# Masked maximum of a graph layer: the own part added graph by graph, the update and the statistics cut in halves, the own products moved to the last selection

## What is computed

```python
m1z = z @ W1.T + b1
m2z = z @ W2.T + b2
pair = relu(m1z[:, :, None, :] + m2z[:, None, :, :])
m = max(where(mask, pair, -inf), axis=2)
x = x + relu(concatenate((z, m), axis=-1) @ Wu.T + bu)
```

## Time and profile before

| | us |
|---|---|
| median of three runs | 2116.69 |
| lowest and highest of them | 2104.98 and 2117.04 |
| the profiled execution | 2111.06 |
| its span | 2109.2 |
| the stretch of `phase_maxpass` from its first `reduce` to its last | 157.06 to 635.93 |

### The profile page before, as it was taken

How to read it: one execution, slowest core, us unless ns; L and a number is a source line. 1 busy time by engine, 2 the same in 40 slices (tenths; PEclk the granted TensorE clock), 3 DMA queues, 4 the chain that set the end, 5 groups by cost and what they waited for, 6 DMA issues and landing times. The chain is left out here.

```text
span 2109.2 us, 43810 instructions
## 1 busy us (share of the span) xinstructions
PE 1749.2 (83%) x13754; PEld 1106.5 (52%) x13771; DVE 1721.6 (82%) x2689; ACT 1396.4 (66%) x3229; POOL 593.0 (28%) x449
## 2 busy tenths in 40 slices
PE   2967677777776899996899999999999588888886
PEld 1855566566563666665465555555555144444445
DVE  5978888888885777875899999999998577777777
ACT  0533333333334989995588888888888577777774
POOL 1530000000002545443354444544444111111110
PEclk9978988988887999999999999999999899999999
DMA  6000000000000000000255555555555899999993
GB/s 180 1 13 1 1 0 0 0 0 0 0 1 4 7 6 6 4 7 21 81 220 225 223 219 224 219 224 220 226 221 219 324 340 344 344 339 341 338 330 87
DMA packets 123567, 292.98 MB, mean 139 GB/s; under 512 B 21376, under 2 KB 57608, under 8 KB 123288
## 3 DMA queue, kind: packets, MB, share of 16 engines
q1 hardware_dynamic: 106360, 283.37, 36.1%
q10 hardware_dynamic: 16896, 8.39, 1.4%
q0 software_dynamic: 256, 0.56, 0.1%
HBM read 150.45 MB, written 141.82 MB: 139 GB/s over the span
## 5 line engine op out<-in xcount | busy, mean ns | idle before, releaser
L1316 POOL TENSOR_TENSOR pair_ring<-hd 128x2048 f32 (+1 forms) x64 | 269.5, 4212 | 310.7 <-DVE pair_ring L1341 310.7
L1401 ACT ACTIVATE v_hid<-v_psW 128x1024 f32<-128x1024 f32 x256 | 263.4, 1029 | 85.2 <-PE v_psW L1439 85.2
L771 DVE TENSOR_REDUCE m_part<-m_psS 128x128 f32<-128x2048 f32 (+1 forms) x128 | 258.9, 2022 | 74.6 <-PE m_psS L638 74.6
L1337 DVE TENSOR_TENSOR pair_ring<-v_psX,hd 128x2048 f32<-128x2048 f32 x128 | 292.2, 2286 | 17.7 <-PE v_psW L1439 17.6
L1439 PE MATMUL v_psW<-pair_ring,p_w1T 128*64 128x512 f32 x1024 | 288.9, 597 | 0.0
L1404 ACT ACTIVATE v_junk<-v_psW 128x1024 bf16<-128x1024 f32 x256 | 263.3, 1029 | 0.0
L638 PE MATMUL m_psS<-m_onehot,m_tableT 32*128 32x128 f32 x3584 | 156.4, 314 | 125.4 <-DVE m_part L771 119.0
L1439 PE MATMUL v_psW<-pair_ring,l_w1T 128*64 128x512 f32 (+1 forms) x1024 | 252.5, 587 | 0.0
L1430 PE MATMUL v_psW<-p_ends,v_weights 128*64 128x512 bf16 x1536 | 235.2, 381 | 3.2 <-DMA v_fold<-in_c_fold_dram 3.2
L1587 DVE SCALAR_TENSOR_TENSOR pair_ring<-pair_ring 128x1024 f32<-128x1024 f32 x128 | 156.4, 1225 | 65.9 <-ACT pair_ring L1654 65.9
L638 PEld LDWEIGHTS m_psS<-m_onehot,m_tableT 32*128 32x128 f32 x3584 | 132.5, 213 | 145.2 <-issue 76.9
(11 more groups left out here) (260 smaller groups left out, 3360.5 us busy)
## 6 DMA issues: line engine op xcount, KB each, us to landing
pair_hidden<-v_hid SPq DMA_DIRECT2D x256, 512.0 KB, 2.6
pair_ring<-pair_hidden SPq DMA_DIRECT2D x128, 1024.0 KB, 7.4
adj_ring<-in_adj_dram ACTq DMA_DIRECT2D x16, 256.0 KB, 5.7
x_all<-in_x_dram ACTq DMA_DIRECT2D x16, 256.0 KB, 5.8
out_dram<-x_all SPq DMA_DIRECT2D x16, 256.0 KB, 2.3
pair_scores<-s_rot SPq DMA_DIRECT2D x64, 32.0 KB, 5.1
s_fwd<-pair_scores SPq DMA_DIRECT2D x64, 32.0 KB, 5.1
s_wide<-pair_scores SPq DMA_DIRECT2D x64, 32.0 KB, 5.5
```

The costliest lines, as they stand in the source:

```text
L771: nc.vector.tensor_reduce(part[:, i % 2, r, :], psS[:, :, 0:w].rearrange("z q (c i) -> z i q c", i=N), AX.XY, ALU.max).then_inc(reduced, 1)
L1316: nc.gpsimd.tensor_tensor(D[:, home(u, SLABS - 1), :].rearrange("c (h d i) -> c h d i", h=2, i=N), one, far, ALU.subtract).then_inc(psub_d ...
L1337: nc.vector.tensor_tensor(slab(s), own, windows(hd, n, s)[1], ALU.max).then_inc(max_done, 1)
L1401: nc.scalar.activation(hid[:, s, :], psW[:, buf, :], ACT.Identity, accum_out=hsum[:, bass.ds(m, 1)]).then_inc(evacuated, 1)
```

## The change

- `add_own` is done for one graph at a time, behind that graph's `merge` (behind `reduce` 1, 3, 5 and 7) in the same quad, instead of once behind `reduce` 0 of the next quad.
- VectorE's `update` is cut in two halves of 256 columns, behind the LATE tables of `reduce` 4 and 6; the first signals a new semaphore `half_added`, the second `added`.
- `statistics` takes two graphs at a time and moves one quad later: behind `reduce` 0 and 2 of the quad after.
- TensorE's `own` moves from behind `select` 5 to behind `select` 7.
- `quads` writes out four quads instead of two, and loops 6 times over two quads. The end of the phase changes with it.

```diff
-            quad(0, 0, False, True)
-            with eng.Fori(0, QUADS // 2 - 1) as t:
+            quad(0, 0, False, True, False)
+            quad(1, 1, True, True, False)
+            with eng.Fori(0, QUADS // 2 - 2) as t:
                 for u in (0, 1):
-                    quad(2 * t + (u + 1), 1 - u, True, True)
-            quad(QUADS - 1, 1, True, False)
+                    quad(2 * t + (u + 2), u, True, True, True)
+            quad(QUADS - 2, 0, True, True, True)
+            quad(QUADS - 1, 1, True, False, True)
...
-                        if at == 5:
+                        if at == 7:
                             own(g, p)
...
-                def add_own(g, p):
-                    dve.wait_ge(merged, done(g * G + (G - 1)))
-                    dve.wait_ge(mT_ready, done(g - 1))
-                    nc.vector.tensor_tensor(both[:, :], mx[:, :], m1[:, p, :], ALU.add).then_inc(summed, 1)
-
-                def update(g):
+                def add_own(g, p, i):
+                    dve.wait_ge(merged, done(g * G + i))
+                    if i == 0:
+                        dve.wait_ge(m1_copied, done(g))
+                        dve.wait_ge(mT_ready, done(g - 1))
+                    last = nc.vector.tensor_tensor(both[:, b(i)], mx[:, b(i)], m1[:, p, b(i)], ALU.add)
+                    if i == G - 1:
+                        last.then_inc(summed, 1)
+
+                def update(g, half):
                     dve.wait_ge(u_mm, done(g))
-                    xs = k.x[:, bass.ds(g * QC, QC)]
-                    nc.vector.scalar_tensor_tensor(out=xs, in0=psU[:, :], scalar=0.0, in1=xs, op0=ALU.max,
-                                                   op1=ALU.add).then_inc(added, 1)
-
-                def statistics(g):
-                    dve.wait_ge(added, done(g))
-                    ln_stats(nc, k, g)
+                    at = half * (QC // 2)
+                    xs = k.x[:, bass.ds(g * QC + at, QC // 2)]
+                    nc.vector.scalar_tensor_tensor(out=xs, in0=psU[:, at:at + QC // 2], scalar=0.0, in1=xs, op0=ALU.max,
+                                                   op1=ALU.add).then_inc(added if half else half_added, 1)
+
+                def statistics(g, half):
+                    dve.wait_ge(added if half else half_added, done(g))
+                    for i in (2 * half, 2 * half + 1):
+                        nc.vector.bn_stats(k.stats[:, bass.ds(g * G + i, 1), :], k.x[:, bass.ds((g * G + i) * C, C)])
...
                         if at == 0:
-                            if prev:
-                                add_own(g - 1, 1 - p)
                             tables(g, p, 2, LATE)
+                            if older:
+                                statistics(g - 2, 0)
                         if at == 1:
                             merge(g, 0)
                             tables(g, p, 3, EARLY)
+                            add_own(g, p, 0)
                         if at == 2:
                             tables(g, p, 3, LATE)
+                            if older:
+                                statistics(g - 2, 1)
...
                         if at == 4:
-                            if prev:
-                                update(g - 1)
                             if next:
                                 tables(g + 1, 1 - p, 0, LATE)
+                            if prev:
+                                update(g - 1, 0)
                         if at == 5:
                             merge(g, 2)
                             if next:
                                 tables(g + 1, 1 - p, 1, EARLY)
+                            add_own(g, p, 2)
+                        if at == 6:
+                            if next:
+                                tables(g + 1, 1 - p, 1, LATE)
                             if prev:
-                                statistics(g - 1)
-                        if at == 6 and next:
-                            tables(g + 1, 1 - p, 1, LATE)
+                                update(g - 1, 1)
...
-                add_own(QUADS - 1, 1)
-                update(QUADS - 1)
-                statistics(QUADS - 1)
+                for half in (0, 1):
+                    statistics(QUADS - 2, half)
+                for half in (0, 1):
+                    update(QUADS - 1, half)
+                for half in (0, 1):
+                    statistics(QUADS - 1, half)
```

More of the change, by code:

```diff
@@ L544, in phase_maxpass @@
             "grown", "tabled", "t_turned", "tT_ready", "match_mm", "onehot_ready"))
-        selected, reduced, merged, summed, mT_ready, own_mm, u_mm, added = (sem(n) for n in (
-            "selected", "reduced", "merged", "summed", "mT_ready", "own_mm", "u_mm", "added"))
+        selected, reduced, merged, summed, mT_ready, own_mm, u_mm, half_added, added = (sem(n) for n in (
+            "selected", "reduced", "merged", "summed", "mT_ready", "own_mm", "u_mm", "half_added", "added"))
         b = lambda i: slice(i * N, (i + 1) * N)
@@ L654, in update, with quad @@
                     last.then_inc(u_mm, 1)
-                def quad(g, p, prev, next):
+                def quad(g, p, prev, next, older):
                     for at in range(ITEMS):
@@ L739, in _ @@
             def _(dve):
-                for s in (tabled, reduced, merged, summed, added):
+                for s in (tabled, reduced, merged, summed, half_added, added):
                     dve.sem_inc(s, BIAS)
@@ L778, in merge, with quad @@
                     nc.vector.tensor_tensor(mx[:, b(i)], part[:, i % 2, 0, :], part[:, i % 2, 1, :], ALU.max).then_inc(merged, 1)
-                def add_own(g, p):
-                    dve.wait_ge(merged, done(g * G + (G - 1)))
-                    dve.wait_ge(mT_ready, done(g - 1))
-                    nc.vector.tensor_tensor(both[:, :], mx[:, :], m1[:, p, :], ALU.add).then_inc(summed, 1)
-                def update(g):
-                    dve.wait_ge(u_mm, done(g))
-                    xs = k.x[:, bass.ds(g * QC, QC)]
-                    nc.vector.scalar_tensor_tensor(out=xs, in0=psU[:, :], scalar=0.0, in1=xs, op0=ALU.max,
-                                                   op1=ALU.add).then_inc(added, 1)
-                def statistics(g):
-                    dve.wait_ge(added, done(g))
-                    ln_stats(nc, k, g)
+                def add_own(g, p, i):
[7 more added lines that the diff above has]
+                def update(g, half):
+                    dve.wait_ge(u_mm, done(g))
+                    at = half * (QC // 2)
[6 more added lines that the diff above has]
+                        nc.vector.bn_stats(k.stats[:, bass.ds(g * G + i, 1), :], k.x[:, bass.ds((g * G + i) * C, C)])
                 EARLY, LATE = range(BLK - 2), range(BLK - 2, BLK)
-                def quad(g, p, prev, next):
+                def quad(g, p, prev, next, older):
                     for at in range(ITEMS):
@@ L813, in quad @@
                                 tables(g + 1, 1 - p, 0, EARLY)
+                            add_own(g, p, 1)
                         if at == 4:
-                            if prev:
-                                update(g - 1)
                             if next:
                                 tables(g + 1, 1 - p, 0, LATE)
+                            if prev:
+                                update(g - 1, 0)
                         if at == 5:
@@ L830, in quad @@
                                 tables(g + 1, 1 - p, 2, EARLY)
+                            add_own(g, p, 3)
                 for i in range(2):
```

## The result

The changed kernel takes 2118.57 us (median of 16 runs), the kernel before 2108.92 (16 runs by then, 7.8 us under the median of the first three). The ratio is 1.0049, with a 95% interval of 1.0028 to 1.007: half a per cent slower. The forecast was a small gain. The time lies in the range, the direction is wrong. One later execution of the kernel before took 6273.40 us, three times the others, and stands in no ratio.

A forecast was written before the change was run, and what follows sets the result against it. The prediction took the loop between `select` and `reduce`, and the clock, as the bound. Terms -2.1 - 2.1 - 2.1 - 0.6 = -6.9 us gave 2104 from the profiled execution or 2110 from the median; it took 2110, range 2086 to 2128.

The forecast's parts named there:

- Step 0: VectorE in step 0: `add_own` out (0.60 us), two `bn_stats` in (0.45); -2.1 us, GpSimd meeting's 0.85 us left in.
- Quarter additions and halves: VectorE: quarter additions hidden in steps 1, 3, 5, 7 (+16 us if not); half `update`s about 0.35 us each.
- Step 4: With half an `update`, step 4 becomes select-bound at 3.44 us: 48.2 against 50.26, -2.1 us.
- Step 5: Without `own`: 8 of 14 at 4.15 us, 6 at 3.21; 52.5 us against 70.12.
- Own at full clock and its wait: Step 7 with `own`: 3.50 us at full clock, plus 0.35 waiting for the second half of `update`: 3.85.
- Own at low clock: Step 7 with `own`: 5.04 + 0.35 = 5.40 us in 10 of 14, 3.85 in 4; 69.4 us against 53.92.
- the last rival: `own` wholly at low clock in every quad: step 7 at 6.66 us, +18 more, kernel 2145 us; chance 0.05.
- The rival that named the low clock throughout steps 5 to 7: Clock low in steps 5 to 7 of each quad: 4.15 + 4.05 + 5.40, 190.4 us, kernel 2127; chance 0.16.

The follow-up runs named there:

- the idle products: Changed kernel plus three unread bf16 products of 512 columns behind `prepare` in each of steps 4, 5 and 6: 2083.20 us, ratio 0.9881 to the kernel before.
- `own` alone: Kernel before with one edit, `own` behind `select` 7 instead of `select` 5: 2124.17 us, ratio 1.0062.
- the wide bias product: Changed kernel with `own`'s bias product over all 128 rows (identity times bias) instead of one row: 2118.24 us, ratio 1.0046.
- the half `update` ahead: Changed kernel with the second half of `update` ahead of the LATE tables behind `reduce` 6: 2116.62 us, ratio 1.0022.
- all but `own`, `update` ahead: Changed kernel with `own` back behind `select` 5 and `update` whole, ahead of the LATE tables behind `reduce` 4: 2102.58 us, ratio 0.9964.
- before with idle products: Kernel before plus three unread bf16 products of 512 columns behind `prepare` in each of steps 4, 6 and 7: 2077.42 us, ratio 0.9846.

## Why the prediction was wrong

**The bound** (the loop of `select` and `reduce`, and the clock) was read rightly; the idle products show that the clock alone is worth 35 us of stretch in the kernel before.

**Step 0.** Forecast 57.4, measured 54.62 us: `add_own` went out as said, and less time was lost beside GpSimd than the 0.85 us I had left in: in the quad at 305.85 the LATE tables take 1.38 us, 0.54 over their 0.84. Step 3 fell by 1.3 us, unforeseen and not explained here.

**Quarter additions and halves.** Right: they are hidden. In the changed kernel VectorE is busy 2.88 of 3.13 us in step 3, and the version with everything but the move is faster than before. The Trainium skill, "VectorE: DVE Perf Modes", section on the TRN2 errata, advises against small tiles; by its formula a quarter takes 291 ns. The trace agrees with the length, 286 ns on average, but no cost of it is exposed here.

**Step 4.** Forecast 48.2, measured 51.20. The step is select-bound as said, and with the idle products it takes 48.20; but the low clock reaches back into `select` 5. I had let the fall start only in step 5.

**Step 5.** Forecast 52.5, measured 53.68. The nearness is in part luck: 11 of 14 were slow, not 8, and both lengths came out shorter than taken (up to 4.06 instead of 4.15, 3.14 instead of 3.21). The share was too low here as well.

**Own at full clock and its wait.** Right in both: 3.50 forecast, 3.60 measured; 0.35 and 0.37 for the wait.

**Own at low clock: the step that failed.** The prediction put "10 slow of 14" at 5.40, 69.4 us. It was 14 of 14 at a mean of 5.79, 81.00 us, and this 11.6 us is more than the whole forecast gain. Two terms are in it.

The share: I counted the clock's falls from a kernel with one light step ahead of `own` and carried the count over, with a little off, to one with three. The text said that the cover was thinner and then took a lower share than the 12 of 14 it had read; the rows gave no reason for that. Four more slow steps are 4 x 1.55 = 6.2 us. Whether more light steps raise the share stays open: with three of them it was 14 of 14 in the changed kernel, but 12 in each of the versions with `own` alone, the wide bias product and the half `update` ahead.

The length, 0.39 us more each on average, 5.5 us in all. Eight of the 14 lie at the usual 5.57 us, which is near the 5.40: with the idle products the same step takes 3.97 and not 3.85 at full clock, and the low clock adds 1.60 and not 1.55. The other six, at 5.78 to 6.37 us and granted clocks of 0.55 to 0.60, ran the whole of `own` at the low clock: its two parts took 1.91 to 1.94 and 2.08 us there, against 1.12 and 1.47 in the quad at 305.85. They alone bring 4.1 of the 5.5 us. That is the step of the last rival (6.66), which stood at 0.05 since it wanted in every quad what two of 14 did; the sum held it in none.

The rival that named the low clock throughout steps 5 to 7 came nearest: 190.4 forecast for their sum, 186.70 measured. It was given 0.16. Its sum is near by errors that cancel: 58.1 for step 5, 56.7 for step 6 and 75.6 for step 7, where 53.68, 52.02 and 81.00 were measured. Its ground was misread too: the two slow steps of the earlier trace rows don't follow two light ones, since step 5 ahead of them holds `own`, with TensorE busy for all of its 5.07 us. Its time of 2127 was too high because it started from the first median, 2116.69. The same start flatters the forecast: counted from 2108.92 it would have been 2102, not 2110.

**The rest of the span.** Of the 11.2 us between the two profiled executions 7.6 lie elsewhere, which the sum didn't hold.

## What to carry to other kernels

Work that is moved to another step is still worth its time at the clock that it meets. Look at the steps ahead of its new place, and where the trace shows the clock low behind steps with little TensorE work, take the low price for every round, not a share.

Where TensorE waits for another engine in each round, try a small idle product in its gap before reordering anything: one of 0.22 us in three of eight steps took the changed kernel from 0.5% slower than before to 1.4% faster, while the best reordering without such products gained 0.36%.

While the clock still falls, a shorter path isn't sure to be shorter time. Taking a wait of `own` away brought 12 us of stretch in one version and none that could be told in another; with the clock held it brought 5.1. When one part of a change is undone, see that the wait it brought goes too.

## What the runs showed of the hardware

The clock makes time of its own, away from the edit. The phase that prepares the pairs, which the change doesn't touch, took these two windows, before and after:

```profile
974.10:1025.90 51.80, 37.01 (x232) 27.77 (x240) 32.54 (x79) 26.32 (x64) 16.66 (x16) 0.92 0.06 20
```

```profile
977.70:1037.10 59.40, 45.26 (x240) 33.02 (x240) 32.53 (x79) 26.33 (x64) 16.59 (x16) 0.77 0.05 18
```

The same instructions, VectorE, ScalarE and GpSimd busy for the same time, and 7.6 us apart at clocks of 0.92 and 0.77. In the other versions it took 51.6 to 51.8 us (six of them, among them all but `own`, `update` ahead), 55.4 to 55.6 (three, among them `own` alone) or 59.4 (before with idle products), by no order that follows their edits. All that lies outside the stretch, the profiled time less the stretch, comes to 1629.9 to 1641.6 us over the twelve kernels. Single executions of one kernel differ by 16 to 29 us here (2104.26 to 2129.94 changed, 2095.25 to 2123.82 before in one of its later rounds), so a difference of a few us had to be read in the stretch and in its steps, not in the span.
